# Two transformer layers: one merged order for both, and three-term fp32r products in place of fp32 ones

## The chip, the cores and the metric

One core of a Trainium2 chip. TensorE (PE) multiplies, VectorE (DVE), ScalarE (ACT) and GpSimd (POOL) work on elements, SyncE (SP) issues the transfers. The metric is the device time of one execution in microseconds, as the median of several runs; lower is better.

## The reference

```python
x = x + L0_attn(layernorm(x))   # 16 query heads, one shared key/value head, plain softmax
x = x + L0_ffn(layernorm(x))    # x rounded to fp8, one 256 x 256 product, bias
x = x + L1_attn(layernorm(x))   # 16 heads, causal, scores + slope * (key - query)
x = x + L1_ffn(layernorm(x))    # x @ (W + up_aux @ lora_up @ lora_down @ down_aux).T + b
```

x is 32 batches of 512 tokens with 256 features in fp32. A head has 16 features (DH), so a score product contracts over 16 values alone.

## The kernel before, in words

The reference's L0 is here called layer 1 (function `layer_mqa`), its L1 is layer 2 (function `layer`). The kernel runs `layer_mqa` over all 32 batches, writes x_mid to memory, and then runs `layer`, in a block of its own with buffers of its own.

Both work in the same way. Batch by batch, `body(b)` is written out for b from -2 to 33; a body works on several batches at once: exponentials for batch b, maxima for heads two quads ahead (so up to batch b + 1), projections for b + 1 and b + 2, the finish for b - 1 and b - 2. A quad is four heads. For a head, four max tiles compute the scores with queries on the partitions; VectorE takes each row's maximum out of a bank (L666; L1559 with the causal mask added). For a quad the negated maxima are split in two bf16 parts (`mparts`), transposed (task m), copied (`mrows`) and sent by DMA as two more rows of the query operand. Then four exp tiles compute the scores transposed, with the maximum already subtracted; ScalarE takes the exponential into `probs` (L564, L1416). The product with the values (PV, L468 and L1295) sums in one bank in column groups of 32, with a column of ones for the sum. Tasks do the rest: otr and ont transpose the result, out multiplies by w_o, xt transposes the normalised input, qk, kv and v project, ft and ffn are the second half of the layer.

Precision of the score products: fp32 values are written as a sum of parts. In layer 1 two fp32r parts stand in three blocks of 16 rows (`Q_TERMS`, `K_TERMS`), 48 rows, 50 with the maxima. Heads 0 to 7 lie in partitions 0 to 63 of `q_op` and `k_op`, heads 8 to 15 in 64 to 127, and since the maxima run eight heads ahead, the max tile and the exp tile of a pair lie in different halves. In layer 2 three bf16 parts stand in six blocks (`Q_PARTS`, `K_PARTS`), with three rows for the position bias, 99 rows, 101 with the maxima. The causal mask is added by a second matmul into the same bank (L1277). Query and key parts go from GpSimd through memory (`qk_parts`) to their place: the store has all heads on the partitions, the loads put 16 features on 16 partitions.

The projections (w_qk, w_v, w_o, in layer 2 w_f too) are plain fp32 matmuls, which the trace shows as two records each.

What sets the order: in layer 1 a plan written by hand, `PLAN_MQA`, read from left to right; each P is a pair, each V a PV tile of a quad, the rest tasks with their number and the batch relative to b. In layer 2 the lists `TASKS` and `ORDER`. Each engine runs its own part of the order strictly; SP and GpSimd have lists of their own in `body`. PSUM banks: layer 1 has 3 for maxima, 4 shared by exp tiles and tasks, 1 for PV; layer 2 has 3, 2 for exp tiles, 2 for tasks, 1. Most buffers are double.

## Time and profile before

| | us |
|---|---|
| median of 3 runs | 3888.25 (3883.73 to 3889.77) |
| the profiled execution, its own time | 3863.94 |
| its span, first to last instruction | 3862.2 |
| TensorE busy in the span | 3636.8 (94%) |
| VectorE, ScalarE, GpSimd busy | 2936.6, 2471.1, 1717.7 |

The rows further down come from the profiled execution. In a row of the timeline stand the start and the duration in us, then engine, line of the kernel, operation, the tile written and those read, and the shapes; x8 means eight instructions merged. Matmuls overlap, so the time that one takes from its followers is the distance of two starts, not its duration.

### The profile page before, as it was taken

What the parts mean: (1) busy time and instruction counts of PE and PEld (TensorE: products, weight loads), DVE (VectorE), ACT (ScalarE), POOL (GpSimd) and SP (SyncE); (2) the same over time, 40 slices, a digit from 0 to 9 for tenths busy, and PEclk for the clock granted to TensorE, in tenths of its full rate; (3) what the DMA queues carried; (4) which work ended last, traced back from release to release, by engine and by line L of the source; (5) the groups of instructions that cost most, each with busy time, mean ns of one, the idle gap of its engine ahead of it and who ended that gap; (6) DMA issues with size and microseconds to landing.
All of it is one profiled execution on the core that took longest, in us unless ns stands there. A gap on an engine that the chain in (4) does not pass through costs nothing. (4 is left out here: it accounts for less than half of the span.)

```text
span 3862.2 us, 76074 instructions
## 1 busy us (share of the span) xinstructions
PE 3636.8 (94%) x25352; PEld 1854.5 (48%) x25352; DVE 2936.6 (76%) x8436; ACT 2471.1 (64%) x5347; POOL 1717.7 (44%) x1956
## 2 busy tenths in 40 slices
PE   5999999999999999998289999999999999999997
PEld 2344444444444444444145555555555555555554
DVE  4899999989998999995076776777767767777664
ACT  2777777777787777776055555555555555555554
POOL 1255555554555555554433343442433434424331
PEclk7999999999999999999599999999999999999999
DMA  3334333333333333331375755756657557566570
GB/s 70 73 77 87 80 90 76 83 79 91 76 82 88 85 84 81 83 74 37 72 120 89 127 104 96 122 105 105 115 93 124 106 94 125 104 103 116 94 122 23
DMA packets 323077, 352.93 MB, mean 91 GB/s; under 512 B 28101, under 2 KB 277371, under 8 KB 322683
## 3 DMA queue, kind: packets, MB, share of 16 engines
q1 hardware_dynamic: 320641, 347.01, 47.6%
q8 instruction: 206, 3.38, 0.4%
q14 instruction: 182, 1.49, 0.2%
q10 hardware_dynamic: 2048, 1.05, 0.1%
HBM read 221.08 MB, written 117.44 MB: 88 GB/s over the span
## 5 line engine op out<-in xcount | busy, mean ns | idle before, releaser
L666 DVE TENSOR_REDUCE maxima<-ps_vector 128x1 f32<-128x512 f32 x2048 | 1282.8, 682 | 162.0 <-PE ps_vector L435 155.6
L1559 DVE CUSTOM_DVE_ANT_0 ps_max<-ps_max,mask 128x128 f32<-128x128 f32 (+3 forms) x2048 | 987.2, 508 | 531.4 <-PE ps_max L1258 512.7
L1416 ACT ACTIVATE probs<-ps_exp 128x512 f32<-128x512 f32 (+3 forms) x2048 | 823.1, 441 | 783.6 <-PE ps_exp L1277 716.0
L564 ACT ACTIVATE probs<-ps_scalar 128x512 f32<-128x512 f32 x2048 | 1073.6, 604 | 155.6 <-PE ps_scalar L449 150.8
L435 PE MATMUL ps_vector<-k_op,q_op 48*128 48x512 f32 x2048 | 715.9, 446 | 48.1 <-DVE maxima L666 28.4
L449 PE MATMUL ps_scalar<-q_op,k_op 50*128 50x512 f32 x2048 | 708.1, 441 | 1.0 <-DVE o_rows L730 0.5
L1273 PE MATMUL ps_exp<-q_op,k_op 101*128 101x512 bf16 (+3 forms) x2048 | 614.3, 301 | 25.6 <-ACT probs L1416 18.0
L1258 PE MATMUL ps_max<-k_op,q_op 99*128 99x128 bf16 (+3 forms) x2048 | 619.4, 304 | 19.9 <-DMA k_op<-qk_parts 16.3
L435 PEld LDWEIGHTS ps_vector<-k_op,q_op 48*128 48x128 f32 x2048 | 333.3, 187 | 549.6 <-DVE maxima L666 394.8
L468 PE MATMUL ps_pv<-probs,v_op 128*32 128x512 f32 x4096 | 552.5, 606 | 0.0
L1704 POOL TENSOR_SCALAR neg_mean<-meanvar 128x4 f32<-128x4 f32 x64 | 12.5, 196 | 1092.0 <-issue 784.6
L1277 PE MATMUL ps_exp<-identb,maskb 128*128 128x128 bf16 x2048 | 449.3, 220 | 0.0
L1258 PEld LDWEIGHTS ps_max<-k_op,q_op 99*128 99x128 bf16 x2048 | 199.4, 97 | 389.6 <-DVE maxima L1559 250.5
L1295 PE MATMUL ps_pv<-probs,v_op 128*32 128x512 f32 (+3 forms) x4096 | 381.6, 445 | 1.0 <-ACT oT L1427 0.9
L449 PEld LDWEIGHTS ps_scalar<-q_op,k_op 50*128 50x128 f32 x2048 | 331.6, 185 | 10.1 <-ACT probs L564 4.5
L1559 DVE DVE_READ_ACCUMULATOR2_ANT maxima<- 128x1 f32 x2048 | 289.5, 141 | 0.4
L1273 PEld LDWEIGHTS ps_exp<-q_op,k_op 101*128 101x128 bf16 x2048 | 199.7, 98 | 170.2 <-ACT probs L1416 74.1
L1332 PE MATMUL ps_task<-xT,w_qk 128*128 128x512 f32 x512 | 252.2, 616 | 1.5 <-ACT xT L1486 0.8
L1277 PEld LDWEIGHTS ps_exp<-identb,maskb 128*128 128x128 bf16 x2048 | 201.2, 98 | 52.1
L778 POOL TENSOR_SCALAR neg_mean<-meanvar 128x4 f32<-128x4 f32 x64 | 12.3, 193 | 391.7 <-DVE meanvar L701 373.2
L837 POOL TENSOR_SCALAR magic<-magic 128x1024 f32<-128x1024 f32 x32 | 116.6, 3645 | 88.7 <-DVE magic L711 88.7
L1723 POOL TENSOR_TENSOR qr<-qf,qparts 128x512 f32<-128x512 f32 x128 | 148.2, 1158 | 10.7
(127 smaller groups left out, 5186.0 us busy)
## 6 DMA issues: line engine op xcount, KB each, us to landing
q_op<-qk_parts SPq DMA_DIRECT2D x192, 256.0 KB, 5.9
qk_parts<-qparts SPq DMA_DIRECT2D x128, 384.0 KB, 3.2
q_op<-qk_parts SPq DMA_DIRECT2D x384, 128.0 KB, 6.4
k_op<-qk_parts SPq DMA_DIRECT2D x384, 128.0 KB, 6.9
qk_parts<-qparts SPq DMA_DIRECT2D x64, 512.0 KB, 4.2
xin<-in_x SPq DMA_DIRECT2D x32, 512.0 KB, 4.8
xres<-in_x SPq DMA_DIRECT2D x32, 512.0 KB, 4.6
x_mid<-xo SPq DMA_DIRECT2D x32, 512.0 KB, 3.2
```

Of the source, the lines that this page charges most:

```text
L435: pe.matmul(ps_vector[:, bank_of("vector", "max", k, d, par), :], q_op[rows, cp, h % HALF, i * P:(i + 1) * P], k_op[rows, cp, :], start=Tr ...
L449: pe.matmul(ps_scalar[:, bank_of("scalar", "exp", p, 0, par), :], k_op[at:at + KB, par, T * P:(T + 1) * P], q_op[at:at + KB, par, s % HALF ...
L468: mm = pe.matmul(ps_pv[VW * j:VW * (j + 1), q0:q0 + nq], v_op[:, cp, T, 0, :], probs[:, quad % 2, at:at + nq], start=(T == 0), stop=(T == ...
L564: act.activation(probs[:, quad % 2, at:at + S], ps_scalar[:, bank_of("scalar", "exp", p, 0, par), :], ACT.Exp).then_inc(ps_out["exp"], 1)
L666: dve.tensor_reduce(at, ps_vector[:, bank_of("vector", "max", k, d, par), :], AX.X, ALU.max).then_inc(ps_out["max"], 1)
L1258: pe.matmul(ps_max[:, bank, 0:keys], q_op[0:KA, cp * HEADS + h, i * P:(i + 1) * P], k_op[0:KA, kh, 0:keys], start=True, stop=True).then_in ...
L1273: mm = pe.matmul(ps_exp[:, bank, 0:nq], k_op[0:KB, kh, T * P:(T + 1) * P], q_op[0:KB, par * HEADS + s, q0:q0 + nq], start=True, stop=not C ...
L1277: mm = pe.matmul(ps_exp[:, bank, 0:P], maskb[:, :], identb[:, :], start=False, stop=True)
L1295: mm = pe.matmul(ps_pv[VW * j:VW * (j + 1), q0:q0 + nq], v_op[:, cp, T, quad * QUAD + j if CAUSAL else 0, :], probs[:, quad % 2, at:at + n ...
L1332: mm = pe.matmul(ps[:, :], w_qk[:, kt, k * P:(k + 1) * P], xT[:, cp, kt, :], start=(kt == 0), stop=(kt == KT - 1))
L1416: act.activation(probs[:, quad % 2, at:at + nq], ps_exp[:, bank, 0:nq], ACT.Exp).then_inc(exp_done, 1)
L1559: ins = dve.tensor_tensor_reduce(row, row, mask[:, S - keys:S], 1.0, LOWEST, ALU.add, ALU.max, at)
```

## The change

It does five things.

1. `layer` becomes `layer_causal`, with operands like layer 1's: two fp32r parts in three blocks, 48 rows and 3 for the bias, 51, and 53 with the maxima; heads 8 to 15 in the upper half. Max and exp tiles become pairs. The splitting of q and k takes two instructions in place of four. Masks come first: at a burst's start `put_mask` writes the masks of up to four exp tiles (`start=True`), the exp tiles add to them.
2. Part products in both layers: each projection's weights are cut once in a high and a low fp32r part, its input is cut by GpSimd (`cut_x`, `cut_ont`, `cut_ft`; two instructions for 128 x 512), and three fp32r matmuls (`TERMS`) replace each fp32 one.
3. Layer 2 gets a plan of its own, `PLAN_CAUSAL`, and `PLAN_MQA` is written anew. All engines, SP and GpSimd too, follow the plans.
4. `joint_order` cuts both plans into pieces and sorts them by time, counted in bodies. Layer 2's body b stands at 33 + b, so its bodies -2 and -1 lie beside layer 1's last full body (31) and what follows; layer 1's bodies 32 and 33, which have no exp tiles, are squeezed to 0.6 each. Both layers share the bank rings of 3 and 4.
5. Both layers share one set of buffers (`kit`), most of them single now (xin, xres, o_rows, xo, kvf, the columns that are cut). Layer 2's weights are loaded and cut at the start, at -1.98 and -0.51 of the order, in the space of layer 1's `probs`, parked in memory (`park`), and fetched when layer 1's places are free (`load_first`, `load_late`). Layer 1's first x is loaded ahead of the constants.

```diff
-TASKS = {
-    0: [
...
-BANKS = {0: (2, 3), 1: (2, 3)}
-
-ORDER = {0: 'A0 E0 A1 E1 PV A2 E2 A3 E3', 1: 'A0 E0 A1 E1 PV A2 E2 A3 E3'}
...
+PPP load_x:0:2 store_qk:0:1 qk:0:1
+PPP kv:0:1 split_qk:0:1
+PPP m:1:0 stat2:2:-2 split_kv:0:1 V
+PPP load_m:1:0 stat2:3:-2 norm2:0:-2 V stat1:0:2 over:0:-2 cut_ont:0:-1 V
+PPP stat1:1:2
+V magic:0:-2 PPPP load_res:0:-1 fp8:0:-2 ont:0:-1
+PPP split:2:0 load_q:0:1 otr:2:-1 V otr:3:-1
+P
+PP exponent:0:-2 m:2:0 V V cut_ont:1:-1 v:0:1 load_k:0:1 load_m:2:0
+PPPP V stat1:2:2
+PPP qk:1:1
+PPP V split_qk:1:1 ont:1:-1 stat1:3:2
+load_m:3:0 PPPP norm1:0:2 V split:3:0 cut_x:0:2
+PPP m:3:0 V
+PPPP ft:0:-2 store_qk:1:1 otr:0:0
+PP V
+PPP ffn:0:-2 cut_x:1:2 split:0:1 otr:1:0 out:0:-1
+PPP m:0:1 load_q:1:1 load_m:0:1 V finish:0:-2 stat2:0:-1 ffn:1:-2 xt:0:2 stat2:1:-1 out:1:-1
+PPP xt:1:2 V store:0:-2
+PPP
+V PPPP split:1:1 finish:1:-2 V
+"""
...
+PLAN_CAUSAL = """
+PPP load_x:0:2 m:1:0 V send:1:0 load_op:0:1
+PPP split_qk:2:1 qk:2:1 cut_ont:0:-1 otr:2:-1 store_qk:2:1
+PP V load_res:0:-1
 PPP V
-PPPP split:2:0 V
-PPP ont:0:-1 otr:3:-1
-PP V m:2:0
-PP V exponent:0:-2
-PPP v:0:1 V ont:1:-1
-PPP qk:1:1
-PPP V
-PPPP split:3:0 V
-PPP m:3:0 V
-PPPP otr:0:0 out:0:-1 ft:0:-2
-PPP V
-PPP split:0:1 stat1:1:2 out:1:-1
-PP ffn:0:-2 m:0:1 V ffn:1:-2 stat1:2:2 stat1:3:2 stat2:0:-1 stat2:1:-1
-PPP V otr:1:0
-PPP V xt:0:2 xt:1:2
-PPPP V split:1:1
+V PPPPP ont:0:-1 split:2:0 qk:3:1 store_qk:3:1
+stat1:0:2 PPP stat1:1:2 split_qk:3:1 v:0:1
+PPP stat1:2:2 m:2:0 V
+PP norm1:0:2 load_op:1:1 otr:3:-1 stat1:3:2 send:2:0 cut_ont:1:-1 v:1:1
+PPP V V V
+PPPP ont:1:-1 V
+PPPP xt:0:2 out:0:-1 store_qk:0:2
+PPP out:1:-1 xt:1:2 V split:3:0 cut_x:0:2 stat2:0:-1 stat2:1:-1 cut_x:1:2
+PPP m:3:0 stat2:2:-1 send:3:0
+PP stat2:3:-1 V otr:0:0 qk:0:2
+PP V
+PPP otr:1:0 qk:1:2
+PPP norm2:0:-1 ft:0:-1 split:0:1 V
+PPPP bias:0:-1 V
+PPPP split_qk:0:2 ft:1:-1 m:0:1
+PP V cut_ft:0:-1 cut_ft:1:-1 send:0:1
+PPP split:1:1 V store_qk:1:2 store:0:-1 ffn:0:-1 ffn:1:-1 split_qk:1:2
 """
 
 
-BANKS_MQA = (3, 4)
+MAX_BANKS, REST_BANKS = 3, 4
+JOIN = 1.0
+TAIL = 0.6
+
...
+def pieces(L, plan):
+
+    cut, burst = [], False
+    for step in plan:
+        if step[0] == "pair":
+            if not burst:
+                cut.append([])
+            burst = True
+        elif step[0] == "pv" or step[0] in PER[L]:
+            cut.append([])
+            burst = False
+        if not cut:
+            cut.append([])
+        cut[-1].append(step)
...
+def joint_order(NB, pairs, ahead_pairs):
+
+    entries = [
+        (-1.98, 1, 0, [("raw", 0, 0)]), (-0.51, 1, 0, [("lora", 0, 0)]),
+        (NB - 1 + 0.02, 1, 0, [("first", 0, 0)]), (NB + 0.01, 1, 0, [("aux", 0, 0)]), (NB + 0.02, 1, 0, [("aux", 1, 0)]),
+        (NB + 0.2, 1, 0, [("clear", 0, 0)]),
+        (NB + 2 * TAIL, 1, 0, [("clear", 1, 0)]), (NB + 2 * TAIL, 1, 0, [("late", 0, 0)]),
+    ]
+    for L, text, start in ((0, PLAN_MQA, 0.0), (1, PLAN_CAUSAL, NB + JOIN)):
+        cut = pieces(L, read_plan(text))
+        for b in range(-2, NB + 2):
+            seen = 0
+            for steps in cut:
+                at = b + seen / pairs
+                if L == 0 and at > NB:
+                    at = NB + (at - NB) * TAIL
+                entries.append((start + at, L, b, steps))
+                seen += sum(step[0] == "pair" for step in steps)
+    entries.sort(key=lambda entry: entry[0])
+    banks, last = {}, {}
+    slots = {"max": 0, "rest": 0}
+
+    def place(ring, size, L, kind, c, k):
+        n = slots[ring] % size
+        slots[ring] += 1
+        banks[L, kind, c, k] = n, last.get((ring, n))
+        last[ring, n] = L, kind, c, k
+
+    for _, L, b, steps in entries:
+        for kind, k, d in steps:
+            if kind == "pair":
+                p = (k + ahead_pairs) % pairs
+                c = b + (k >= ahead_pairs)
+                if 0 <= c < NB:
+                    place("max", MAX_BANKS, L, "max", c, p)
+                if 0 <= b < NB:
+                    place("rest", REST_BANKS, L, "exp", b, k)
+            elif kind in PER[L] and 0 <= b + d < NB:
+                place("rest", REST_BANKS, L, kind, b + d, k)
+    return [entry[1:] for entry in entries], banks
 
 
...
+    TERMS = [(kt, xp, wp) for kt in range(KT) for xp, wp in ((0, 0), (0, 1), (1, 0))]
...
+                pe.wait_ge(x_cut, KT * (c + 1))
+                for n, (kt, xp, wp) in enumerate(TERMS):
+                    mm = pe.matmul(ps[:, :], w_qk[:, wp, kt, k * P:(k + 1) * P], xT[:, xp, kt, :],
+                                   start=(n == 0), stop=(n == len(TERMS) - 1))
+            elif kind == "kv":
...
+        def cut_x(c, k):
+
+            if not valid(c):
+                return
+            n = KT * c + k
+            if k == 0:
+                if due(seen := per["v"] * c):
+                    pool.wait_ge(ps_full["v"], seen)
+                    pool.wait_ge(ps_full["qk"], per["qk"] * c)
+                else:
+                    pool.wait_ge(ahead["ps_full"]["kv"], NB)
+                    pool.wait_ge(ahead["ps_full"]["qk"], PER[0]["qk"] * NB)
+            pool.wait_ge(ps_out["xt"], n + 1)
+            settled()
+            pool.tensor_scalar(xT[:, 0, k, :], x_cols[:, :], 1.0, 0.0, ALU.mult, ALU.add).then_inc(x_step, 1)
+            pool.wait_ge(x_step, n + 1)
+            pool.tensor_tensor(xT[:, 1, k, :], x_cols[:, :], xT[:, 0, k, :].bitcast(F32),
+                               ALU.subtract).then_inc(x_cut, 1)
...
+        def load_first():
+
+            sp.wait_ge(parked["stored"], 16)
+            sp.wait_ge(ahead["ps_full"]["qk"], PER[0]["qk"] * NB)
+            sp.wait_ge(ahead["ps_full"]["v"], NB)
+            sp.wait_ge(ahead["ps_full"]["kv"], NB)
+            for unit in range(2):
+                sp.wait_ge(ahead["op_loaded"][unit], 16 * UNIT_LOADS * NB)
+            fetch(w_qk, at_qk, NQK * P).then_inc(first_in, 16)
+            fetch(w_v, at_v, D).then_inc(first_in, 16)
...
+        def load_late():
+
+            sp.wait_ge(ahead["ps_full"]["ffn"], 2 * NB)
+            sp.wait_ge(ahead["o_ready"], 2 * NB)
+            fetch(w_o, at_o, D).then_inc(late_in, 16)
+            fetch(w_f, at_f, D).then_inc(late_in, 16)
+            sp.dma_start(bias[:, :], consts["bias"]).then_inc(late_in, 16)
+
...
+            for g in range(len(Q_TERMS)):
+                at = HALF_ROWS * unit + g * DH
+                src = qk_dram[par, Q_TERMS[g], 2 * unit, :, :]
+                sp.dma_start(q_op[at:at + DH, par, :, :].bitcast(F32),
+                             src.rearrange("(h d) s -> d h s", d=DH)).then_inc(op_loaded[unit], 16)
+                src = qk_dram[par, K_TERMS[g], 2 * unit + 1, :, :]
+                sp.dma_start(k_op[at:at + DH, par, :, :].bitcast(F32),
+                             src.rearrange("(h d) s -> d h s", d=DH)).then_inc(op_loaded[unit], 16)
...
+        def put_mask(p, b, par):
+
+            if not valid(b):
+                return
+            wait_bank(pe, "exp", b, p)
+            pe.matmul(ps_rest[:, bank("exp", b, p), 0:P], maskb[:, :], identb[:, :],
+                      start=True, stop=False, skip_group_check=True)
+
+        def exp_tile(p, b, par):
+
+            if not valid(b):
+                return
+            s, T = divmod(p, NT)
+            if T == 0 and s % QUAD == 0:
+                pe.wait_ge(m_loaded, 16 * M_ROWS * (b * NQUAD + s // QUAD + 1))
+            at = HALF_ROWS * (s // HALF)
+            q0, nq = span(T)
+            pe.matmul(ps_rest[:, bank("exp", b, p), 0:nq],
+                      k_op[at:at + KB, par, s % HALF, T * P:(T + 1) * P],
+                      q_op[at:at + KB, par, s % HALF, q0:q0 + nq],
+                      start=False, stop=True, skip_group_check=True).then_inc(ps_full["exp"], 1)
...
+        def token_rows(ps, cols, w, k):
+
+            for t in (2 * k, 2 * k + 1):
+                for n, (kt, xp, wp) in enumerate(TERMS):
+                    mm = pe.matmul(ps[:, (t % 2) * D:(t % 2 + 1) * D], cols[:, xp, kt, t * P:(t + 1) * P],
+                                   w[:, wp, kt, :], start=(n == 0), stop=(n == len(TERMS) - 1))
+            return mm
...
+        def body(b, par, steps):
+            masked = None
+            burst = [k for kind, k, d in steps if kind == "pair"]
+            for kind, k, d in steps:
+                if kind == "pair":
+                    if masked is None or masked == k:
+                        for p in burst[burst.index(k):burst.index(k) + REST_BANKS]:
+                            put_mask(p, b, par)
+                            masked = p + 1
+                    max_tile(k, b, par)
+                    exp_tile(k, b, par)
...
+        def cut_weights():
+
+            steps = [0]
+
+            def link(ins):
+
+                steps[0] += 1
+                ins.then_inc(parked["cut"], 1)
+                dve.wait_ge(parked["cut"], steps[0])
+
+            dve.wait_ge(raw_in, 16 * 8)
+            dve.wait_ge(lora_pe, 3)
+            link(dve.tensor_tensor(whole_f, ps_pv[:, 0:KT * D], whole_f, ALU.add))
+            for at, one in ((at_qk, whole_qk), (at_v, whole_v), (at_o, whole_o), (at_f, whole_f)):
+                n = one.shape[1]
+                hi, lo = parts[:, 2 * at:2 * at + n], parts[:, 2 * at + n:2 * at + 2 * n]
+                link(dve.tensor_scalar(hi.bitcast(F32R), one, 1.0, 0.0, ALU.mult, ALU.add))
+                link(dve.tensor_tensor(lo.bitcast(F32R), one, hi, ALU.subtract))
...
+        def in_order(*bodies):
+
+            for L, b, steps in order:
+                bodies[L](b, b % 2, steps)
 
```

## Rows read from the trace of the kernel before

**Rows 1.** Windows by stage: length, busy us (count) by engine, clock, DMA share, GB/s.

```profile
71.00:1802.00 1731.00, 1681.02 (x11090) 745.64 (x11090) 1549.38 (x3098) 1354.24 (x2633) 907.10 (x906) 0.99 0.37 80
1802.00:1955.00 153.00, 61.05 (x218) 30.38 (x217) 30.62 (x110) 18.09 (x30) 69.04 (x72) 0.61 0.36 68
1955.00:3824.00 1869.00, 1841.59 (x13866) 1048.46 (x13865) 1321.21 (x5147) 1087.41 (x2664) 722.75 (x947) 1.00 0.61 106
1000.00:1200.00 200.00, 195.88 (x1311) 86.92 (x1312) 181.25 (x365) 158.19 (x309) 112.06 (x109) 1.00 0.39 86
2600.00:2800.00 200.00, 197.72 (x1494) 113.92 (x1494) 144.17 (x560) 115.37 (x283) 81.92 (x107) 1.00 0.67 116
```

The engines stand in the order PE, PEld (weight loads), DVE, ACT, POOL.

**Rows 2.** Order of time on TensorE, layer 1: start, duration.

```profile
1002.39 0.50 PE L435 MATMUL ps_vector<-k_op,q_op 48*128 48x512 f32 x1
1002.39 0.50 PE L449 MATMUL ps_scalar<-q_op,k_op 50*128 50x512 f32 x1
1002.73 0.39 PE L435 MATMUL ps_vector<-k_op,q_op 48*128 48x512 f32 x1
...
1002.96 0.39 PE L435 MATMUL ps_vector<-k_op,q_op 48*128 48x512 f32 x1
...
1003.28 0.33 PE L487 MATMUL ps_scalar<-identb,mparts 128*8 128x128 bf16 x3
...
1021.86 1.98 PE L504 MATMUL ps_scalar<-xT,w_qk 128*128 128x512 f32 x4
1023.77 0.50 PE L435 MATMUL ps_vector<-k_op,q_op 48*128 48x512 f32 x1
```

**Rows 3.** Order of time on TensorE, layer 2.

```profile
2619.97 1.94 PE L1343 MATMUL ps_task<-w_v,xT 128*128 128x256 f32 x8
2621.75 0.22 PE L1258 MATMUL ps_max<-k_op,q_op 99*128 99x128 bf16 x1
2621.81 0.38 PE L1273 MATMUL ps_exp<-q_op,k_op 101*128 101x512 bf16 x1
2622.03 0.22 PE L1277 MATMUL ps_exp<-identb,maskb 128*128 128x128 bf16 x1
2622.08 0.27 PE L1258 MATMUL ps_max<-k_op,q_op 99*128 99x256 bf16 x1
...
2622.51 0.43 PE L1295 MATMUL ps_pv<-probs,v_op 128*32 128x128 f32 x8
2622.87 0.34 PE L1258 MATMUL ps_max<-k_op,q_op 99*128 99x384 bf16 x1
...
2623.55 0.60 PE L1324 MATMUL ps_task<-ident,o_rows 128*128 128x128 f32 x4
```

**Rows 4.** Weight loads by line, layer 1, 1000 to 1200 us: busy, mean ns, idle.

```profile
L435 PEld LDWEIGHTS ps_vector<-k_op,q_op 48*128 48x128 f32 x241 | 38.5, 184 | 63.2 <-DVE maxima L666 47.2 <-issue 9.8 <-DMA q_op<-qk_parts 2.3
```

**Rows 5.** Waits, 2600 to 2800 us: total, times, longest us.

```profile
PEld ps_max L1258 <- DVE maxima L1559: 26.1, 44, 0.8
```

**Rows 6.** GpSimd by line, layer 1, 1000 to 1200 us.

```profile
L797 POOL TENSOR_TENSOR qparts<-qf,qparts 128x512 fp32r<-128x512 f32 x8 | 10.2, 1281 | 0.7
...
L795 POOL TENSOR_SCALAR qparts<-qf 128x512 fp32r<-128x512 f32 x8 | 5.0, 623 | 11.6 <-ACT qf L621 11.6
```

**Rows 7.** Weight loads by line, layer 2, 2600 to 2800 us.

```profile
L1273 PEld LDWEIGHTS ps_exp<-q_op,k_op 101*128 101x128 bf16 x218 | 21.3, 98 | 16.9 <-ACT probs L1416 6.9 <-issue 4.6
```

**Rows 8.** Windows while operands are loaded, layer 1 and layer 2.

```profile
1016.00:1020.00 4.00, 4.00 (x38) 1.61 (x33) 3.96 (x8) 3.11 (x7) 1.17 (x2) 1.00 1.07 157
2608.00:2616.00 8.00, 7.92 (x61) 4.43 (x60) 6.50 (x28) 5.22 (x14) 2.58 (x7) 1.00 1.13 124
```

**Rows 9.** Order of time on TensorE: layer 2's first max tiles.

```profile
1932.92 1.56 PE L1258 MATMUL ps_max<-k_op,q_op 99*128 99x128 bf16 x5 [16.29 <-DMA k_op<-qk_parts]
```

**Rows 10.** Order of time on VectorE, the head.

```profile
12.71 0.69 DVE L122 TENSOR_TENSOR z<-z,magic 128x512 f32<-128x512 f32 x1
...
47.13 12.05 DVE L666 TENSOR_REDUCE maxima<-ps_vector 128x1 f32<-128x512 f32 x20 [25.54 <-PE ps_vector L435]
```

2699 lines of the change are left out of this document (1258 added, 1441 removed).

## The prediction

> **What bounds the kernel now.** I read the windows by stage first [rows 1]. The reader is to see four stretches. Layer 1's scores run from 71 to 1802 us, 1731 us for 32 batches, 54.1 us each. Layer 2's run from 1955 to 3824 us, 1869 us, 58.4 us each. Between them lie 153 us in which no exponential is computed: TensorE is busy for 61 us of them, at a mean granted clock of 0.61. The head is 71 us and the tail, to the end of the 3862 us span, 38 us. 71 + 1731 + 153 + 1869 + 38 = 3862.
>
> In both steady windows of [rows 1] TensorE is busy nearly throughout (195.88 and 197.72 of 200 us). Busy alone could hide waits, so I read the order of time next [rows 2, 3]. In layer 1 a max tile and an exp tile start together, because they lie in different halves of the array's rows, and the pair costs one 0.23 us spacing (1002.73 to 1002.96). In layer 2 the 99-row and 101-row matmuls share the array and follow one another. VectorE is the second limit in layer 1: 181.25 of 200 us, and weight loads of the max tiles waited 47.2 us for its banks [rows 1, 4]. In layer 2 it is busy 144.17 of 200, with 26.1 us of such waits [rows 1, 5]. So layer 2 is set by TensorE alone, layer 1 by TensorE with VectorE close behind, and the 153 us by latency and in-order set-up.
>
> **Layer 1, per batch.** Products with w_qk, w_v and w_o are fp32 matmuls now, two records for each, and become three single-pass fp32r matmuls (high by high, high by low, low by high). A qk task takes 1.91 us (1021.86 to 1023.77) [rows 2]. Afterwards it is six 512-column matmuls at the 0.23 us spacing, plus 0.1 for the first, 1.48 us. That is 0.43 less, twice, and about 0.4 less for kv. An out task is like the layer-2 task of eight 256-column records, 1.78 us (2619.97 to 2621.75) [rows 3]; afterwards it is twelve 256-column matmuls at half the spacing, 0.115 us, plus 0.1, 1.48 us: 0.30 less, twice. Sum 0.86 + 0.4 + 0.6 = 1.9 us less, so 54.1 becomes 52.2. Shorter tasks let VectorE be fed earlier and the waits of [rows 4] shrink, but VectorE's own floor is 181.25/200 of 54.1, 49.0 us. I take 0.5 us for it: 51.7 us. Bounds: 49.5 (VectorE's floor) and 54.1 (no gain). The price of the parts is GpSimd work: four more cuts, each 0.62 + 1.28 us [rows 6], 7.6 us more on an engine that is busy 112.06 of 200 us, 30 of a batch's 54 us [rows 1]. It reaches 38 of 52 us and stays hidden; with the single buffers the next transpose waits for its cut, which is late only if GpSimd falls behind the orders written in the plan.
>
> The 0.115 us rests on the weight load being hidden. An fp32r weight load lasts 184 ns, a bf16 one 98 ns [rows 4, 7], but 184 ns includes its latency; the unhidden extreme is one load and one matmul in series, 0.23 us for each, 2.86 us for each out, v or ffn task. The Trainium skill ("TensorE: Matmul & The Clock Gate", LDWEIGHTS) prices a load of 128 columns at 128/1.2, 107 ns, and says the fast load is off for fp32; by that the two would be level at 256 columns and the task would come to the same 1.4 us. No row here has an fp32r matmul under 512 columns.
>
> **Layer 2, per batch.** First the scores. Between 2621.75 and 2623.55 lies one head, four max tiles, four exp tiles and four masks, with one product with the probabilities from 2622.51 to 2622.87 among them: 1.80 - 0.36 = 1.44 us [rows 3], 16 heads 23.0 us. After the change operands have 51 and 53 rows and are paired as in layer 1. A head's pairs of 512, 384, 256 and 128 columns cost 0.23, 0.17, 0.12 and 0.11 us by the columns, 0.63; 16 heads 10.1 us. A burst of pairs costs more than its spacings: three pairs took 0.89 us (1002.39 to 1003.28), not 0.69 [rows 2]; 21 bursts at 0.20 are 4.2 us. Masks remain, 64 at 0.05 (2622.03 to 2622.08) [rows 3], 3.5 us with one start more a burst. Sum 17.8, 5.2 us less. Then ten projections (four qk, two each of v, out and ffn) at 0.30 less, 3.0 us. 58.4 - 8.2 = 50.2.
>
> Two additions. All masks of a burst now go first, so the first pair waits until ScalarE has emptied up to four banks; behind that wait stand the max tiles too, and VectorE waits for those. ScalarE is busy 115.37 of 200 us [rows 1] and usually has a 1 us product between bursts to catch up: I take 1.1 us (bounds 0 and 5, ten bursts late by 0.5). And a 128-column fp32r matmul may run slower than its columns say; between 0.11 and 0.22 us, the mask's duration, I take half: 0.05 for 16 pairs, 0.8 us. 50.2 + 1.1 + 0.8 = 52.1 us. VectorE's floor, 144.17/200 of 58.4, is 42 us. GpSimd loses eight of sixteen splitting instructions and gains twelve, a few us on 24. Bounds: 49.5 and 57.
>
> Switching between the 64-row and the full array is what the 0.20 us buys. The Trainium skill ("TensorEngine Tiling (Array Packing)", Key Properties) says a mode change drains the engine; the burst row agrees. If each full drain cost 0.16 us (duration 0.39 less spacing 0.23), masks ahead of pairs would add one more per burst, 3.4 us a batch. That is part of the second rival.
>
> **Loads.** Operand bytes stay equal (three terms of 4 bytes for six of 2), in half as many transfers with rows twice as long. Layer 2's loads moved 124 GB/s with the queues full, layer 1's longer rows 157 [rows 8], so a unit's 1.5 MB goes from about 13 to 10 us. It must be in before pair 33, 25 us into the body, and starts some 5 us in (after the last store). Slack about 10 us: free.
>
> **Junction.** Layer 2's first loads, projections and 32 maxima go beside layer 1's last batches. Layer 1's last TensorE work, the FFN chain through GpSimd and the reload of constants no longer stand before it. What stays from the last layer-1 exp tile to the first layer-2 one: unit 0's load, held until the earlier batch is done (in the kernel before, TensorE waited 16.3 us for it [rows 9]), 15 to 20 us; then 32 maxima, 22 us at layer 2's busy share; then split, transpose and send, 4 us; then what layer 1's tail puts between in the same queues, 6 us. I take 50 instead of 153, bounds 40 and 90.
>
> **Head and tail.** VectorE cuts layer 1's weights (1088 columns more, about 3 us) and, at -0.51 of the order, layer 2's 2560 columns twice: at 0.69 us for 512 [rows 10], below 7 us, in the stretch where it reduces the first maxima back to back (20 in 12.05 us). Waits for the small LoRA products sit there too. Nothing covers this, so 71 becomes 80. Tail: 38, cuts added (4 us), projections shorter.
>
> **Sum.** 80 + 32 x 51.7 + 50 + 32 x 52.1 + 38 = 3490 us of span; with 1.7 us around it (3863.94 - 3862.2) 3491. The profiled execution stands 0.63% below the median of the runs (3863.94 to 3888.25), so 3513 us.
>
> **Rivals.**
> 1. VectorE already sets layer 1: it stays at 54. For: 90% busy, 47.2 us of waits on its banks. Against: TensorE is idle even less. + 74 us: 3587.
> 2. Masks first and the extra drains eat the pairing in layer 2: 56 us. For: two modes in every burst. Against: ScalarE has 42% free. + 125: 3640.
> 3. The weight load isn't hidden at 256 columns: 1.38 us more in each of eight tasks a pair of batches, 353 us over 32; no gain is left in layer 2: 3870. Against: loads at 512 columns are fully hidden.
> 4. Slower than before: the operand loads come too late. Unit 0 is needed at pair 33, just over half of the body. Layer 2 must reach 64 us a batch to cancel all gains, so the load must land 34 us after the body's start instead of some 15. For: the last split, the store and twelve sequential steps hang on one queue. Against: the whole 3 MB takes 20 us. About 3950 at 66 us.
> 5. Better: both layers reach their floors, 49.5 and 49.5: 3350.
> 6. The merge doesn't work: an in-order queue waits for layer 1's last store and the junction stays above 110: 3575.
>
> **How the numbers follow.** Forecast 0.50; rival 1, 0.13; rival 2, 0.13; rival 3, 0.04; rival 4, 0.04; rival 5, 0.10; rival 6, 0.06. The range 3380 to 3690 holds the forecast with 1, 2, 6 and part of 5. What a measurement can tell from no change is 0.2%, 8 us. Rival 4 is slower, rival 3 is split about the line: faster 0.92, same 0.02, slower 0.06.
>
> **What would show it.** First and last exp tile of each layer: 51.7 and 52.1 us a batch, 50 us between the layers. Records: a qk task of six in under 1.5 us, a 256-column record every 0.115 us, pairs starting together in layer 2. Wrong if weight loads pace the 256-column tasks, if the first mask of a burst waits on ScalarE, if VectorE's idle share in layer 1 goes to nil (rival 1), or if TensorE waits for a load at pair 33.

## The result, and the profile after

The changed kernel takes 3727.43 us (median of 4 runs, 3721.09 to 3749.69), against 3886.45 before (median of 4 runs on the same chip): a ratio of 0.961, 95% interval 0.958 to 0.965. It is faster, but by 3.9% where 9.6% was forecast, and 3727 lies above the range of 3380 to 3690. The profiled execution has a span of 3729.6 us.

First and last exp tile of each layer cut that span into five parts, against the forecast's terms:

| | before | forecast | measured |
|---|---|---|---|
| head | 71 | 80 | 71.8 |
| layer 1, us a batch x 32 | 54.1 | 51.7 | 55.3 |
| between the layers | 153 | 50 | 64.3 |
| layer 2, us a batch x 32 | 58.4 | 52.1 | 55.6 |
| tail | 38 | 38 | 43.8 |

Layer 1 rose, and layer 2 gained 2.8 us a batch of the 6.3 it was to gain. The two make 116 and 112 of the 240 us by which the span exceeds the forecast's 3490. Not all of layer 1's rise over before is in its loop. Of 1770 us against 1731, 15 lie in the last batch, which takes 61.5 us from its first exp tile to its last, 46.3 before; layer 2's first maxima now stand beside it. The 22 us put on top (profiled execution below the median) weren't there this time.

The windows by stage of the kernel after (busy us and instructions of PE, PEld, DVE, ACT, POOL, then granted clock, DMA share, GB/s), which answer to [rows 1]:

```profile
71.00:1842.00 1771.00, 1658.48 (x11546) 790.17 (x11546) 1595.47 (x3113) 1368.82 (x2637) 1152.34 (x1165) 0.99 0.38 80
1842.00:1906.00 64.00, 39.52 (x196) 26.02 (x194) 25.41 (x93) 11.96 (x20) 44.91 (x46) 0.71 0.67 109
1906.00:3686.00 1780.00, 1715.45 (x14869) 1099.98 (x14868) 1314.12 (x5150) 1096.84 (x2670) 888.48 (x1082) 0.98 0.69 122
1000.00:1200.00 200.00, 188.87 (x1316) 88.69 (x1313) 183.57 (x357) 155.73 (x302) 136.16 (x138) 1.00 0.40 84
2300.00:2500.00 200.00, 196.76 (x1739) 127.88 (x1738) 152.57 (x597) 125.76 (x306) 101.05 (x126) 1.00 0.76 134
```

In layer 1 GpSimd went from 112 to 136 of 200 us, as forecast (38 of 55 us a batch). TensorE's busy time fell from 196 to 189 of 200: it has less to do and waits more. VectorE went up, from 181 to 184 (49.0 to 50.8 us a batch), though the change gives it nothing more to do in layer 1's loop. So I looked at VectorE's instructions first. Here are the two that split the maxima, from 200 to 1800 us; first of the kernel before, then after (count | busy us, mean ns of one | idle before):

```profile
L679 DVE TENSOR_SCALAR mparts<-maxima 128x16 bf16<-128x16 f32 x117 | 46.1, 394 | 1.0
L681 DVE SCALAR_TENSOR_TENSOR mparts<-maxima,mparts 128x16 bf16<-128x16 f32 x117 | 26.7, 228 | 4.0
```

```profile
L692 DVE TENSOR_SCALAR mparts<-maxima 128x16 bf16<-128x16 f32 x116 | 97.3, 839 | 1.0
L694 DVE SCALAR_TENSOR_TENSOR mparts<-maxima,mparts 128x16 bf16<-128x16 f32 x116 | 32.1, 277 | 4.0
```

The same instruction on 16 numbers a partition takes 0.39 us on average before and 0.84 us after. The timeline of the kernel after, one of these splits, shows why:

```profile
649.67 2.13 POOL L886 TENSOR_TENSOR xq<-xq,xn 128x1024 bf16<-128x1024 bf16 x1
...
650.40 1.43 DVE L692 TENSOR_SCALAR mparts<-maxima 128x16 bf16<-128x16 f32 x1
...
651.76 0.62 POOL L804 TENSOR_SCALAR o_cols<-o_half 128x512 fp32r<-128x512 f32 x1
651.86 0.55 DVE L694 SCALAR_TENSOR_TENSOR mparts<-maxima,mparts 128x16 bf16<-128x16 f32 x1
652.33 1.28 DVE L679 TENSOR_REDUCE maxima<-ps_max 128x1 f32<-128x512 f32 x2
...
652.56 0.33 PE L495 MATMUL ps_rest<-identb,mparts 128*8 128x128 bf16 x3 [1.43 <-DVE mparts L694]
```

GpSimd's addition ends at 651.80, VectorE's split at 651.83; GpSimd's next instruction ends at 652.38, VectorE's second at 652.41. Over the 116 splits of this stretch, 86 began while GpSimd was inside a tensor-by-tensor instruction, and these took 1.07 us on average, 85 of them ending within 0.06 us of GpSimd's; the other 30 took 0.17. The reductions out of PSUM took 0.68 us whatever GpSimd did. So the splits, which read and write SBUF, stand still until GpSimd's running instruction is over. The Trainium skill ("SBUF — State Buffer", Who interferes with whom) says that VectorE and GpSimd share one pair of ports, and that VectorE uses it in its 2-port modes, which a tensor_scalar can enter, and, while GpSimd reads, with two inputs from SBUF. In a 2-port mode whichever engine comes first holds the pair for its whole instruction and the other is blocked; a tensor_reduce isn't affected on this chip. The trace agrees, with the 85 of 86 ends above; that the splits run in such a mode is not read from it.

Counting an undisturbed split as 0.17 us for each of its two instructions (0.341 for both), VectorE stood still for (97.3 + 32.1 - 116 x 0.341) / 29 = 3.1 us a batch after, and 1.1 us before. Sorted by what GpSimd was running, 2.0 of the 3.1 us fell beside instructions of the FFN chain, which the kernel before has too (1.0 of its 1.1), and 1.1 beside the new cuts.

The last row of the timeline is what makes it count. Task m of the third quad, which transposes the split, had TensorE idle for 1.43 us. These are TensorE's waits for a split from 200 to 1800 us (total, times, longest), before and after:

```profile
PE ps_scalar L487 <- DVE mparts L681: 11.6, 6, 2.1
```

```profile
PE ps_rest L495 <- DVE mparts L694: 41.6, 29, 1.7
```

In the kernel before, the third quad's split met the FFN chain's last addition (2.13 us; L850, after the change L886) in 6 of 29 batches, and those took 56.2 to 57.6 us instead of 53.8. In the kernel after it meets it in every batch.

In layer 2 the timeline of TensorE after shows what the forecast had built up:

```profile
2401.30 0.40 PE L1251 MATMUL ps_rest<-identb,maskb 128*128 128x128 bf16 x4
2401.63 0.32 PE L1242 MATMUL ps_max<-k_op,q_op 51*128 51x128 f32 x1
2401.63 0.32 PE L1263 MATMUL ps_rest<-q_op,k_op 53*128 53x128 f32 x1
...
2409.12 3.10 PE L1296 MATMUL ps_rest<-w_f,o_cols 128*128 128x256 f32 x24
2412.06 0.34 PE L1251 MATMUL ps_rest<-identb,maskb 128*128 128x128 bf16 x3
2412.33 0.49 PE L1242 MATMUL ps_max<-k_op,q_op 51*128 51x512 f32 x1
...
2415.22 1.68 PE L1330 MATMUL ps_rest<-xT,w_qk 128*128 128x512 f32 x6
2416.74 0.49 PE L1316 MATMUL ps_rest<-ident,oT 128*128 128x128 f32 x3
```

The pairs start together. Two ffn tasks, 24 matmuls of 256 columns, take 2.94 us (2409.12 to 2412.06; forecast 2 x 1.48), a qk task 1.52 (forecast 1.48, before 1.91 [rows 2]): the weight loads are hidden at 256 columns, and rival 3 is out. But a group of four masks takes 0.33 us, one of three 0.27 (distances of starts), where four times 0.05 and three times 0.05 were counted.

### The profile page after: what moved, and what is told of

Same layout as the page of the kernel before. It is cut to its first block and busy times, and to the rows that moved or that the text cites. A ratio compares the mean times of both kernels' runs of the same rounds, so it can differ in the third digit from the quotient of the medians.

```text
span 3729.6 us, 79324 instructions
## 1 busy us (share of the span) xinstructions
PE 3470.8 (93%) x26824; PEld 1953.8 (52%) x26824; DVE 2979.1 (80%) x8450; ACT 2488.9 (67%) x5347; POOL 2120.0 (57%) x2340
## 3 DMA queue, kind: packets, MB, share of 16 engines
q14 instruction: 185, 1.52, 0.2%
## 5 line engine op out<-in xcount | busy, mean ns | idle before, releaser
L679 DVE TENSOR_REDUCE maxima<-ps_max 128x1 f32<-128x512 f32 x2048 | 1272.6, 682 | 85.6 <-PE ps_max L443 81.9
L1520 DVE CUSTOM_DVE_ANT_0 ps_max<-ps_max,mask 128x512 f32<-128x512 f32 (+3 forms) x2048 | 962.8, 516 | 353.4 <-PE ps_max L1242 350.7
L574 ACT ACTIVATE probs<-ps_rest 128x512 f32<-128x512 f32 x2048 | 1073.4, 602 | 243.4 <-PE ps_rest L456 242.7
L1393 ACT ACTIVATE probs<-ps_rest 128x512 f32<-128x512 f32 (+3 forms) x2048 | 773.6, 436 | 457.9 <-PE ps_rest L1263 405.6
L443 PE MATMUL ps_max<-k_op,q_op 48*128 48x512 f32 x2048 | 733.5, 448 | 62.3 <-DVE maxima L679 51.7
L456 PE MATMUL ps_rest<-q_op,k_op 50*128 50x512 f32 x2048 | 734.1, 445 | 0.9 <-DVE o_rows L741 0.5
L443 PEld LDWEIGHTS ps_max<-k_op,q_op 48*128 48x128 f32 x2048 | 341.3, 186 | 544.7 <-DVE maxima L679 447.9
L1242 PE MATMUL ps_max<-k_op,q_op 51*128 51x512 f32 (+3 forms) x2048 | 564.2, 366 | 23.6 <-DVE maxima L1520 4.6
L1263 PE MATMUL ps_rest<-q_op,k_op 53*128 53x512 f32 (+3 forms) x2048 | 558.2, 365 | 26.4 <-DMA q_op<-mrows 24.7
L456 PEld LDWEIGHTS ps_rest<-q_op,k_op 50*128 50x128 f32 x2048 | 337.6, 185 | 17.1 <-DVE o_rows L741 8.7
```

Source lines behind the costliest of these rows:

```text
L443: pe.matmul(ps_max[:, bank("max", c, k), :], q_op[rows, cp, h % HALF, i * P:(i + 1) * P], k_op[rows, cp, :], start=True, stop=True).then_i ...
L456: pe.matmul(ps_rest[:, bank("exp", b, p), :], k_op[at:at + KB, par, T * P:(T + 1) * P], q_op[at:at + KB, par, s % HALF, :], start=True, st ...
L574: act.activation(probs[:, quad % 2, at:at + S], ps_rest[:, bank("exp", b, p), :], ACT.Exp).then_inc(ps_out["exp"], 1)
L679: dve.tensor_reduce(at, ps_max[:, bank("max", c, k), :], AX.X, ALU.max).then_inc(ps_out["max"], 1)
L1242: pe.matmul(ps_max[:, bank("max", c, k), 0:keys], q_op[rows, cp, h % HALF, i * P:(i + 1) * P], k_op[rows, cp, h % HALF, 0:keys], start=Tru ...
L1263: pe.matmul(ps_rest[:, bank("exp", b, p), 0:nq], k_op[at:at + KB, par, s % HALF, T * P:(T + 1) * P], q_op[at:at + KB, par, s % HALF, q0:q0 ...
```

## The experiments

Each is the changed kernel with the edit shown. "Layer 1" and "layer 2" are us a batch, for layer 1 the steady value, for layer 2 the mean of 32. Ratios are to the kernel before, run beside it on the same chip. The experiments ran on five chips, on which the kernel before took 3874 to 3889 us, so small differences between rows are read from the ratios. A run marked "one run" has no interval.

| kernel | us | ratio (95%) | layer 1 | layer 2 |
|---|---|---|---|---|
| changed kernel | 3727 | 0.961 (0.958 to 0.965) | 55.3 | 55.6 |
| hi_one_port | 3726 | 0.960 (0.957 to 0.962) | 55.3 | 55.1 |
| half_maxima_l1 | 3634, one run | | 52.6 | 55.5 |
| one_term_l1 | 3741, one run | | 53.8 and 58.8 | 55.3 |
| one_term_half_l1 | 3482, one run | | 47.8 (mean 48.7) | 54.7 |
| fp32_products_l1 | 3741 | 0.963 (0.960 to 0.965) | 55.6 | 55.8 |
| cut_x_later | 3713 | 0.955 (0.952 to 0.958) | 54.9 | 55.8 |
| exponent_earlier | 3673 | 0.948 (0.946 to 0.951) | 53.5 | 55.4 |
| split_on_gpsimd | 4406 | 1.135 (1.131 to 1.138) | 78.5 | 54.5 |
| gpsimd_holds | 3840 | 0.988 (0.986 to 0.990) | 59 | 56.4 |
| holds_and_sends | 3832 | 0.987 (0.984 to 0.989) | 59 | 55.2 |
| masks_last | 3791 | 0.979 (0.975 to 0.984) | 55.3 | 57.2 |
| mask_pairs | 3784 | 0.978 (0.975 to 0.981) | 55.3 | 57.3 |
| no_masks_l2 | 3712, one run | | 55.3 | 55.0 |
| half_maxima_l2 | 3732, one run | | 55.3 | 55.5 |
| no_masks_half_l2 | 3672, one run | | 55.3 | 53.8 |
| banks_4_3 | 4158 | 1.074 (1.069 to 1.078) | 58.0 | 65.5 |
| banks_2_5 | 4522 | 1.166 (1.162 to 1.170) | 68 | 67.5 |
| layers_apart | 3801, one run | | 55.3 | 55.6 |

### Layer 1: who paces it

**hi_one_port.**

```diff
-dve.tensor_scalar(hi, m, -1.0, None, ALU.mult)
+dve.scalar_tensor_tensor(hi, m, -2.0, m, ALU.mult, ALU.add)
```

> VectorE's first instruction of each split of the maxima (written as -1 times m, one input) is rewritten as (-2 times m) + m, the same value bit for bit, in both layers; nothing else. Theory A (VectorE paces layer 1, and this instruction, 0.86 us in the changed kernel against 0.29 us before, is held up while GpSimd, now 68% busy, is at work): it falls to about 0.25 us, 4 x 0.6 = 2.4 us a batch come off VectorE, layer 1 goes from 55.4 to about 53.3 us a batch, the time from 3727 to about 3655 us. Theory B (TensorE's own order of work, bursts of pairs and three-pass tasks, paces layer 1): the instruction may fall, layer 1 stays at 55.4 and the time within 8 us of 3727. Layer 2 in both: 54 to 55 us a batch, since VectorE has slack there.

```profile
L692 DVE SCALAR_TENSOR_TENSOR mparts<-maxima 128x16 bf16<-128x16 f32 x116 | 98.4, 848 | 1.0
```

The instruction takes 0.85 us in its new form too, and layer 1 doesn't move. This was my first version of theory A, which blamed the one-input form; it fell. Which of the two forms VectorE uses makes no difference; when it is issued does, as cut_x_later and exponent_earlier show.

**half_maxima_l1, one_term_l1, one_term_half_l1.** The first cuts `ps_max[...]` to `0:S // 2` in the reduction, the second `TERMS` to `((0, 0),)`, the third does both.

> VectorE's maxima of layer 1 look at the first 256 of 512 keys only (the other half of each row is left out of the maximum); TensorE's matmuls are untouched. It takes about 0.25 us off each of 64 reductions, 16 us a batch of VectorE. Theory A: layer 1 falls from 55.4 to TensorE's own floor, which I put at about 50 us (its records start to start less the waits for banks), so some 170 us less in all. Theory B: layer 1 stays above 54 us a batch.

> Layer 1's products with w_qk, w_v and w_o take the high-by-high term only (both products with low parts are left out); GpSimd's cuts stay. It takes 2 x 4 + 4 of the 512-column matmuls (12 x 0.23) and 16 of the 256-column ones (16 x 0.12), about 4.7 us a batch, off TensorE. Theory A: layer 1 stays within 1 us of 55.4 us a batch, the time above 3690 us. Theory B: layer 1 falls to about 51 us, the time to about 3580 us.

> Layer 1 with both reliefs together: VectorE's maxima look at the first 256 of 512 keys (the other half is left out), and its products with w_qk, w_v and w_o take the high-by-high term only. Alone the first gave 52.6 and the second 53.8 (at full clock) us a batch instead of 55.3. Theory T: together they give more than the sum of both (2.7 + 1.5), because each engine was what the other waited for: 52.6 less the whole 4.7 us of TensorE, about 48 us a batch where the granted clock stays at 1.00. Theory G (a third thing, GpSimd's or ScalarE's chain, stands close behind): it stays above 50 us a batch at full clock.

The window from 1000 to 1200 us of half_maxima_l1:

```profile
1000.00:1200.00 200.00, 194.14 (x1388) 92.47 (x1384) 137.96 (x379) 163.03 (x318) 147.16 (x146) 1.00 0.39 84
```

Taking 17 us a batch off VectorE (64 reductions, 0.27 us less in each) gives 2.7 us, not the 5 that theory A had expected: with VectorE busy 138 of 200 us, a batch still takes 52.6 us. Relieving TensorE of 4.7 us gives at best 1.5 (53.8), and about every second batch takes 58.8. Both reliefs together give 47.8 us in most batches: 52.6 less 4.7, as theory T said. So neither engine paces layer 1 alone, and a saving on one of them is passed on in part. That they take turns, VectorE short of filled banks during TensorE's tasks and TensorE short of empty ones within a burst, is my reading of this. The wait before task m has a share in it: it was 1.4 us in the changed kernel, 2.0 in one_term_l1 and gone in one_term_half_l1.

The batches of 58.8 us in one_term_l1 come with a lower clock. Windows of four microseconds, the granted clock third from the end:

```profile
1072.00:1076.00 4.00, 2.83 (x14) 1.10 (x10) 3.96 (x7) 3.54 (x7) 3.77 (x5) 0.90 0.06 20
1076.00:1080.00 4.00, 4.00 (x22) 1.57 (x20) 3.19 (x6) 3.20 (x6) 2.52 (x3) 0.50 1.00 277
1080.00:1084.00 4.00, 4.00 (x27) 1.24 (x22) 2.36 (x5) 1.57 (x3) 0.10 (x1) 0.75 0.65 209
1084.00:1088.00 4.00, 3.58 (x27) 1.33 (x23) 3.95 (x11) 3.29 (x7) 3.08 (x7) 1.00 1.08 167
```

TensorE was busy 2.83 of 4 us, then the granted clock fell to 0.5 (1.2 GHz) and came back some 7 us later. From 200 to 1800 us the clock was at 0.5 for 208 us, against 3 us in the changed kernel. So work taken off TensorE while VectorE was busy nearly throughout came back here as a slower TensorE. No run separates the clock from the rest of the 5 us between 53.8 and 58.8.

**fp32_products_l1.** Layer 1's `TERMS` has one term (the low parts are left out), operands are read as fp32, ScalarE writes the transposed input straight into its place, and `cut_x` and `cut_ont` are gone.

> The part products are undone in layer 1 alone: its products with w_qk, w_v and w_o are fp32 matmuls again, on operands that hold the high part only (the low parts are left out), and GpSimd's four cuts a batch are gone (7.6 us). TensorE has about 1.3 us a batch more in these tasks, GpSimd 7.6 us less, so VectorE's splits meet it less often. Theory A': VectorE paces layer 1 and gains from GpSimd's rest; layer 1 falls to about 54 us a batch, as before the change, time about 3690 us. Theory B: layer 1 rises from 55.3 to 56.6 us a batch, time about 3770 us.

```profile
L692 DVE TENSOR_SCALAR mparts<-maxima 128x16 bf16<-128x16 f32 x115 | 43.8, 381 | 1.0
L694 DVE SCALAR_TENSOR_TENSOR mparts<-maxima,mparts 128x16 bf16<-128x16 f32 x115 | 30.8, 268 | 3.9
```

Layer 1 stands at 55.6. TensorE's qk, kv and out tasks take 1.5 us a batch more (from the starts of their records: 9.4 against 7.9 us), VectorE stands still for 1.2 us instead of 3.1, and the two cancel. In this order of work the part products bought layer 1 nothing.

Neither theory's number came (54 and 56.6), and the miss of the first says more than the two that cancel. Tasks and GpSimd's work are here as in the kernel before, and so is the time for which VectorE stands still (1.1 us there), yet the batch is 1.1 us longer (54.5 to 55.6, batches 3 to 29). The cuts can't be the reason, since there are none. What is left is the new plan with its buffers. One part of it is in the trace: the third quad's split meets the FFN chain's last addition in every batch here too, and TensorE waits for it (200 to 1800 us):

```profile
PE ps_rest L495 <- DVE mparts L694: 28.5, 28, 1.2
```

**cut_x_later and exponent_earlier.** The first moves `cut_x:0:2` and `cut_x:1:2` behind `xt:0:2` and `xt:1:2` in the plan. The second does so too and moves VectorE's instruction that GpSimd's FFN chain waits for three pairs up (three, not the four of the expectation):

```diff
-PPP split:2:0 load_q:0:1 otr:2:-1 V otr:3:-1
+PPP split:2:0 load_q:0:1 otr:2:-1 V otr:3:-1 exponent:0:-2
...
-PP exponent:0:-2 m:2:0 V V cut_ont:1:-1 v:0:1 load_k:0:1 load_m:2:0
+PP m:2:0 V V cut_ont:1:-1 v:0:1 load_k:0:1 load_m:2:0
```

> GpSimd's two cuts of layer 1's transposed input stand in the written order right behind the transposes that they wait for, instead of some pairs ahead of them (where GpSimd stood waiting with other work behind it). Nothing else. It is the control of the run with GpSimd's split, and shifts the times at which GpSimd's tensor-by-tensor instructions run against VectorE's splits. Theory A' (three of four splits of the maxima in layer 1 stand still until GpSimd's running tensor-by-tensor instruction ends, whatever VectorE's own form): the mean of the first split instruction moves with the number of such meetings, and layer 1 moves with it, by VectorE's gain: four meetings fewer or more of about 0.8 us are at most 3 us a batch; I expect layer 1 between 53.5 and 56.5 us a batch. Theory B (TensorE's own order paces layer 1): 55.3 whatever the meetings.

> On top of the run with the later cuts: VectorE's instruction that the FFN chain of layer 1 on GpSimd waits for stands 4 pairs earlier in the written order, so GpSimd's chain of 11.5 us starts some 2 us earlier, and the two meetings a batch that are left (with the subtraction of a cut and with the chain's last addition, 0.65 and 1.25 us) shift. Theory A': layer 1 moves by the change of VectorE's stood-still time, at most 0.9 of it: 53.8 us a batch (time about 3680) if both meetings go, 55.3 (3730) if there are three again. Theory B: 54.9 us a batch whatever the meetings.

The two groups of cut_x_later, then of exponent_earlier:

```profile
L692 DVE TENSOR_SCALAR mparts<-maxima 128x16 bf16<-128x16 f32 x117 | 76.5, 654 | 1.0
L694 DVE SCALAR_TENSOR_TENSOR mparts<-maxima,mparts 128x16 bf16<-128x16 f32 x116 | 31.0, 267 | 4.0
```

```profile
L692 DVE TENSOR_SCALAR mparts<-maxima 128x16 bf16<-128x16 f32 x117 | 42.6, 364 | 1.0
L694 DVE SCALAR_TENSOR_TENSOR mparts<-maxima,mparts 128x16 bf16<-128x16 f32 x117 | 20.5, 175 | 4.0
```

No instruction was added or taken away, only the order of GpSimd's work against VectorE's. The five kernels side by side, us a batch, means of batches 3 to 29 (tasks are qk, kv and out; pairs include the waits behind them, that before task m too):

| | layer 1 | VectorE stands still | TensorE waits for a split | tasks | pairs |
|---|---|---|---|---|---|
| before | 54.5 | 1.1 | 0.4 | 9.3 | 22.1 |
| fp32_products_l1 | 55.6 | 1.2 | 1.0 | 9.4 | 23.8 |
| changed kernel | 55.4 | 3.1 | 1.4 | 7.9 | 25.1 |
| cut_x_later | 55.1 | 2.3 | 1.4 | 7.9 | 24.7 |
| exponent_earlier | 53.5 | 0.8 | none | 7.9 | 23.2 |

cut_x_later takes away the meeting that nobody waits for directly: 0.8 us less of standing still, some 0.4 us of layer 1. exponent_earlier takes away the one in front of task m: 1.5 us less of standing still, 1.4 us less wait, 1.4 us of layer 1 (54.9 to 53.5). So the time for which VectorE stands still isn't a price by itself (compare the first two rows); what TensorE waits for is. GpSimd's chain also starts earlier in exponent_earlier, but TensorE doesn't wait for GpSimd in layer 1 in either trace. exponent_earlier went past its expected 53.8, and at 0.948 (0.946 to 0.951) it beats both kernels.

**split_on_gpsimd and gpsimd_holds.** Two attempts to take the meetings away altogether. The first, on top of cut_x_later, moves `split_maxima` to GpSimd, as three instructions. The second, on top of exponent_earlier, lets GpSimd wait for VectorE's split, in the plan's row 7, and moves `cut_ont:0:-1` there from row 4:

```diff
-PPP split:2:0 load_q:0:1 otr:2:-1 V otr:3:-1
+PPP split:2:0 hold:2:0 cut_ont:0:-1 load_q:0:1 otr:2:-1 V otr:3:-1 exponent:0:-2
...
+if kind == "hold":
+    pool.wait_ge(m_split, (b + d) * NQUAD + k + 1)
```

> As the control, and the splits of the maxima move from VectorE to GpSimd in both layers, as three small instructions there (some 0.2 us each). VectorE then has no instruction left in the loops that reads two operands from SBUF or copies SBUF to SBUF, but one of 0.68 us a batch. Theory A': 3.4 + 1.1 = 4.5 us a batch come off VectorE in layer 1 (50.8 to 46.3), no meeting is left, and layer 1 falls to about 53 us a batch, near the 52.6 that half of the maxima gave; time about 3650 us. Rival E: the splits now queue behind GpSimd's 1.3 to 3.6 us instructions, the rows of maxima come too late for the exponentials, and TensorE waits instead: layer 1 at 56 us or more, layer 2 above 56, time above 3750 us.

> On top of the run with the earlier exponent: GpSimd waits for VectorE's split of the third quad of maxima before it starts the cut that this split still met (0.65 us once a batch). VectorE's stood-still time falls from 0.77 to about 0.1 us a batch; nothing of TensorE's or VectorE's own order changes. Theory A' with the slope that the other runs gave (0.8 us of layer 1 for each us of standing still): layer 1 from 53.45 to about 52.9 us a batch, time from 3673 to about 3656 us. Theory B (the earlier runs gained by GpSimd's chain starting earlier, not by the meetings): layer 1 stays at 53.45 us, time within 6 us of 3673.

Both failed. The kernel gives GpSimd its work in a fixed order, and one instruction of it lasts up to 3.6 us, so what stands behind comes late. With the splits there (rival E), layer 1 takes 78.5 us; the granted clock was lower as well, 0.89 over the span, and the two weren't separated. In gpsimd_holds the splits met nothing (mean 0.17 us), but I had put the cut behind `fp8` in the plan, so that it ran after the whole FFN chain. ScalarE's next copy then waited for the buffer, and TensorE for that copy (waits from 1000 to 1200 us of gpsimd_holds):

```profile
ACT o_half L632 <- POOL o_cols L806: 14.5, 3, 4.9
PE ps_rest L456 <- ACT o_half L632: 10.1, 3, 3.4
```

So the last 0.7 us a batch of standing still was not tested by itself: the run shows the price of a late cut (and of a clock of 0.954 over the span, against 0.977), not the absence of a meeting.

### Layer 2: masks, turns and sends

**masks_last and mask_pairs.** The pairs of a group go before its masks (`start=True` moves to the score tile); the slice `+ REST_BANKS` becomes `+ 2`.

> In layer 2 each group of up to four score tiles puts its pairs first and its masks last, where the changed kernel puts the masks first; the same number of matmuls and of changes between full and half array. Theory C (masks first make the head of a burst wait until ScalarE has emptied up to four banks; the masks' weight loads waited 16.2 us of 200 us for it, 4.4 us a batch): the banks are asked for one at a time, behind max tiles, and layer 2 falls from 54.5 to about 51.5 us a batch, the time from 3727 to about 3640 us. Theory D (the masks cost what the full array's turn costs, whichever end of the burst they stand at): within 1 us a batch of 54.5, the time within 20 us of 3727; it may be slower, since ScalarE gets its tiles later.

> In layer 2 the masks go ahead of their tiles in groups of up to two instead of up to four: shorter waits for ScalarE's banks, some ten changes between full and half array a batch more. Theory C (the wait for up to four banks is what masks first cost): layer 2 falls by 1 us a batch or more, time 3695 us or less. Theory D (the turns cost, some 0.1 us each, the waits nothing): layer 2 rises by about 1 us a batch, time about 3760 us.

Both are slower, by some 1.7 us a batch, so theory C (waiting for four banks) is out. Theory D has the right direction and is too small: it had allowed about 1 us. TensorE's timeline of mask_pairs shows the price of a turn:

```profile
2400.96 0.29 PE L1251 MATMUL ps_rest<-identb,maskb 128*128 128x128 bf16 x2
2401.18 0.33 PE L1242 MATMUL ps_max<-k_op,q_op 51*128 51x128 f32 x1
...
2401.72 0.23 PE L1251 MATMUL ps_rest<-identb,maskb 128*128 128x128 bf16 x1
2401.88 0.43 PE L1242 MATMUL ps_max<-k_op,q_op 51*128 51x384 f32 x1
```

A group of one, two, three and four masks takes 0.16, 0.22, 0.27 and 0.33 us: 0.055 for each mask and 0.11 for the group. With the 22 groups of `PLAN_CAUSAL` that is 64 x 0.055 + 22 x 0.11 = 5.9 us; the trace has 6.3. mask_pairs has 38 groups, and its steady batch takes 56.6 us against 54.1 to 54.7: 2.2 us for 16 turns, 0.14 each. The records of its masks account for 1.4 of the 2.2 us (7.7 against 6.3); that the rest is pairs starting late behind a turn is my reading.

**no_masks_l2, half_maxima_l2, no_masks_half_l2.** In the first, `put_mask` isn't called, the exp tile waits for its bank itself, and both masks are zero. In the second the reduction reads `1:keys:2`. The third does both.

> Layer 2 without the causal mask inside its diagonal blocks: the 64 mask matmuls a batch are left out, and VectorE adds zeros in place of its mask (same instructions). Theory C (the masks and the turns between half and full array that they bring, and the waits for up to four banks ahead of a burst, are what makes layer 2's scores 23.3 us a batch instead of 17.8): TensorE loses the masks' 6.4 us a batch, and layer 2 falls from 54.5 to about 48.5 us a batch, time about 3535 us. Theory D (another engine or the banks of the maxima hold layer 2 close behind): layer 2 stays above 52 us a batch.

> VectorE's maxima of layer 2 look at every second key only (the others are left out), so its 64 reductions a batch shorten by up to 0.25 us each, some 10 us of its 42. TensorE's matmuls are untouched. Theory D2 (in layer 2 TensorE alone is the bound: 98% busy at clock 1.00, waits for VectorE's banks 9.8 of 200 us, which the masks' waits for ScalarE would take over): the steady batch falls by less than 1 us from 54.6. Theory T2 (the two take turns in layer 2 too, which is why leaving out 6.3 us of masks brought nothing): it falls by 2 us or more, the time by 60 us or more.

> Layer 2 with both reliefs: its mask matmuls are left out (no causal mask inside the diagonal blocks) and its maxima look at every second key only. Alone the first left the batches between 52.7 and 57 us (mean 55.0), the second at 53.6. Theory T2 (TensorE and VectorE take turns, as in layer 1, where both reliefs together gave 47.8 as summed): 54.6 less the masks' 6.3 us, about 48 us a batch, time about 3520 us. Theory L (the rows of maxima, sent by DMA behind 3 MB of operand loads a batch, come no sooner, so TensorE waits for them): above 52 us, with the waits of the score tiles for these sends grown to several us a batch.

VectorE isn't the bound: with 9 us a batch less of it, the steady batch goes from 54.1 to 53.6. But without the masks, 6.3 us of TensorE, layer 2 still takes 55.0, and with both reliefs 53.8 (51.8 at the least). Waits for weight loads from 2300 to 3300 us in no_masks_l2, then the windows of the changed kernel, no_masks_l2 and no_masks_half_l2:

```profile
PEld ps_max L1242 <- DVE maxima L1520: 155.4, 357, 1.2
PEld ps_rest L1264 <- DMA q_op<-mrows: 38.9, 28, 3.2
```

```profile
2300.00:3300.00 1000.00, 968.64 (x8457) 625.57 (x8456) 749.98 (x2941) 617.98 (x1504) 511.01 (x628) 0.99 0.71 125
```

```profile
2300.00:3300.00 1000.00, 931.24 (x7470) 581.44 (x7469) 754.19 (x2998) 619.55 (x1538) 524.09 (x641) 0.98 0.72 127
```

```profile
2300.00:3300.00 1000.00, 929.05 (x7591) 583.82 (x7590) 589.43 (x3053) 623.02 (x1560) 527.70 (x649) 0.98 0.74 130
```

TensorE is idle for some 70 us of 1000 in both, and its work costs more: in no_masks_l2, between batches 8 and 24, the v, out and ffn matmuls stand 134 ns apart instead of 129, the PV ones 89 instead of 83. What is left is a mixture: waits for VectorE's maxima, for sends (39 us of 1000, 2 us a batch), and the lower clock (0.98 against 0.99). I can't give the shares; no run took the sends or the clock away by themselves. Theory L holds for its part only, and T2's 48 us is refuted: both reliefs together gave 1.8 us. So something else stands close behind the masks, and it stays open.

**holds_and_sends.** Five of the changed kernel's batches behind the second took 58.6 to 61.0 us, and in each the first exp tile of the second quad had waited 2.6 to 3.6 us for its maxima, as here:

```profile
2807.29 0.50 PE L1242 MATMUL ps_max<-k_op,q_op 51*128 51x512 f32 x1
2811.43 0.79 PE L1263 MATMUL ps_rest<-q_op,k_op 53*128 53x512 f32 x1 [3.63 <-DMA q_op<-mrows]
```

On top of gpsimd_holds, `load_op:0:1` moves from behind `send:1:0` to behind `otr:2:-1`.

> As the run where GpSimd holds, and in layer 2 the first operand load of a batch is issued 3 pairs and two tasks later, behind the send of the second quad's maxima instead of beside it. If the slow batches are this send queued behind that load (its score tile is the one that waited, 3 to 4 us), they go, and layer 2's mean falls from 55.4 to about 54.6 us a batch: 20 to 25 us less, time about 3635 us. If the load is then late for the maxima of the second half of the batch (needed at pair 33, about 21 us behind the new issue), TensorE waits there instead and layer 2 rises above 56 us.

Against gpsimd_holds, waits above 1.5 us at that tile fell from 11 batches to 3, and layer 2 from 56.4 to 55.2 us a batch. That fits sends queueing behind the operand load, but doesn't show it. The same count is 5 in the changed kernel and 3 in hi_one_port, which leaves loads and sends as they were, and each count is of one execution. The medians differ by 7 us (3840 and 3832), within the spread of either. It wasn't combined with exponent_earlier alone.

### Banks and the merge

**banks_4_3 and banks_2_5.** `MAX_BANKS, REST_BANKS = 4, 3` and `2, 5`.

> Both layers: the maxima get four PSUM banks and everything else three, instead of three and four (in layer 2 masks then go in groups of up to three). The same instructions otherwise. Theory T (TensorE and VectorE take turns: during TensorE's tasks VectorE runs out of filled banks, during a burst TensorE runs out of empty ones, so that neither is busy throughout and a saving on one is passed on in part): a fourth bank lets both run on, layer 1 falls from 55.3 to 54 us a batch or less unless ScalarE's banks, now three, take the wait over; time about 3690 us. Theory B (TensorE's own order alone): no change in layer 1. Rival: the exponentials are short of banks, the time rises above 3750 us.

> Both layers: the maxima have two PSUM banks and everything else five, instead of three and four. With four and three the time rose by 12% over the changed kernel, since the scores' banks ran short (layer 1 58.0, layer 2 64.1 us a batch). If the ring of everything else is the scarce one in layer 2 (its masks wait for banks that ScalarE has yet to empty), layer 2 falls below 54 us a batch. Layer 1, where VectorE is 92% busy, gets fewer filled banks in store: 57 us or more. Time about 3760 us, with the two layers moving in opposite directions; if layer 2 doesn't fall, both rings are at their best as they are.

Both are far slower in both layers, so three and four is the best of the three splits tried. With two banks for the maxima TensorE waits for VectorE: from 2300 to 3300 us the weight loads of the max tiles waited 241 us for maxima, against 47 us in the changed kernel. With three for the rest layer 2 is hit hardest (65.5), presumably because masks and exponentials come short; I didn't find the wait that grew. Theory T's gain from a fourth bank didn't show.

**layers_apart.** `JOIN = 3.2` in place of 1.0.

> Layer 2's order starts 3.2 batches behind layer 1's instead of 1.0: nothing of layer 2 stands beside layer 1's batches, all else is equal (weights still parked and cut at the start, part products in both layers). If the merged order is what shortened the stretch between the last exponential of layer 1 and the first of layer 2 from 153 to 64 us, that stretch grows back to 120 to 150 us and the time by 60 to 90 us, to 3790 to 3820 us. If other parts did it (weights cut and constants loaded beforehand): below 100 us, time below 3765 us. Layers 1 and 2 themselves stay at 55.3 and 54.6 us a batch in both cases; if layer 2's first batches (65.8, 57.7 us in the changed kernel) fall to 55 us, the merge had charged 14 us there.

```profile
1831.00:1977.00 146.00, 53.42 (x232) 36.03 (x230) 30.21 (x106) 16.86 (x27) 69.86 (x69) 0.60 0.48 88
```

The stretch between the layers grows to 146 us (64.3 in the changed kernel, 152.5 before) and layer 1 ends 11 us sooner: 73 us more in all, in one run. The merged order is what shortened it. Layer 2's first two batches stay long (61.1 and 65.0 us), so the merge doesn't charge them. What it charges is layer 1's last batch: 48.5 us from first to last exp tile here, 61.5 in the changed kernel.

## Why the prediction missed

The direction was right, and so were the head (71.8, against 71 before; the weight cuts were hidden after all), the projections' 0.115 us for 256 columns (0.12 measured), the pairs in layer 2, the loads (no wait at pair 33; rival 4 is out), the junction within its bounds (64 for 50) and that rival 6 wouldn't happen.

**Layer 1, the step that failed.** "It reaches 38 of 52 us and stays hidden": GpSimd's load was forecast rightly, but it was not hidden. I had costed GpSimd's work by GpSimd's idle time alone, and had asked only whether its results come in time, not whom its instructions hold up while they run. VectorE's splits stand still beside them for 3.1 us a batch instead of 1.1, and TensorE waits 1.4 us in every batch in front of task m of the third quad, where it had waited in 6 of 29. The hint was in the trace of before: an instruction whose shortest time is 0.16 us takes 0.39 on average. The order alone gave 1.8 us back (exponent_earlier, 53.5). Only some 0.4 us of that wait goes with the new cuts. The addition that the split meets is an old one, and fp32_products_l1, which has no cuts, waits 1.0 us there. It is the new plan that makes them meet in every batch, and the forecast gave the new plan of layer 1 no price at all.

The second step is "1.9 us less" with 0.5 on top for shorter waits. The tasks got 1.4 us shorter (9.3 to 7.9 us), and the waits grew instead: pairs with their waits went from 22.1 to 25.1 us a batch. exponent_earlier takes 1.9 of these 3.0 us away. The last 1.1 us, there with VectorE nearly full and the tasks shorter, is not explained by any run; VectorE as the next limit behind TensorE would look like this. The floor of 49.0 was never near: with VectorE well relieved the layer takes 52.6. Rival 1 named VectorE and 54 us; it had the engine, and not the reason for which it would get worse. Outside the loop, the maxima of layer 2 that go beside layer 1's last batch cost it 13 us (61.5 against 48.5 in layers_apart), which the forecast had put at nothing.

**Layer 2, the term that was mis-sized.** Masks at 0.05 each with "one start more a burst", 3.5 us, and 1.1 us for waiting on ScalarE: measured 6.3, and not by waiting (mask_pairs, masks_last). It is the turn between half and full array, 0.11 us for each group and more behind it, which stood in the prediction as 0.16 us inside rival 2 and not in the sum. The 0.05 was read off a single distance; the kernel before spent 0.08 on each of its masks on average. Pairs came to 16.8 us in the steady batches (records start to start) instead of 14.3 + 0.8. That is 3.4 us too little in the scores, set against 2.5 us between 54.6 and 52.1; another 1.0 lies between 54.6 and the mean of 55.6, in the first two batches (65.8 and 57.7 us) and in five slow ones, where TensorE waits for a send. But sizing the masks rightly would not have been enough. Without them layer 2 still takes 55.0 us (no_masks_l2), so the forecast's 52.1 lacked a second limit as well; which one stays open.

**The chances.** Rivals 1 and 2, at 13% each, together give 3513 + 74 + 125 = 3712 us, and something like both happened. That the measured 3727 is near this sum is luck in part: layer 1 went to 55.3, above rival 1's 54, and layer 2 stayed below rival 2's 56. The range was made by taking the cases one at a time; two that are independent and each more likely than 1 in 10 have to be added as well.

## What to carry to other kernels

Work put on an idle GpSimd isn't free while VectorE is nearly full: a small SBUF-to-SBUF instruction of VectorE may stand still for the rest of GpSimd's running one. So look up its shortest and its mean duration before you add to GpSimd or reorder it. Then find the meeting that another engine waits behind, and move the two apart in the order, which alone gave 1.3% here. Where two engines feed each other through three or four banks, don't forecast by the floor of either: 17 us off VectorE's reductions came back to a sixth, 4.7 us off TensorE to a third, and with VectorE relieved TensorE's 4.7 came back in full. When a mode of the array changes inside a loop, count the changes as well as the instructions. And when a sum closes, try it on the run that undoes the suspected cause: fp32_products_l1 undid the cuts and layer 1 didn't return to 54.

## What was not expected of the hardware

- A VectorE instruction of 0.17 us took up to 1.73 us, ending with GpSimd's (2.1 us in the kernel before). Beside a tensor-by-scalar instruction of GpSimd the second split took 0.55 us, so both kinds hold it up.
- A group of n masks (full array, 128 columns) between half-array pairs took 0.11 + 0.055 n us.
- The granted clock fell to 0.5 for some 7 us after 4 us in which TensorE was busy 2.83, in a kernel with less TensorE work (one_term_l1); its batches went from 53.8 to 58.8 us and back.
- TensorE waited up to 3.6 us for an 8 KB send that was issued among six operand loads; that the loads held it up is likely and not shown.
